# Layer 1 of a graph attention network: ELU from two Relus, softmax denominators over 125 partitions, last head in two pieces

## The reference

```python
h = (layernorm(x) @ W1).reshape(n, 8, 96)
e = leaky_relu(al_s[src] + al_d[dst], 0.2)
ex = exp(e - m[dst])                       # m: largest e into a node
z = segment_sum(ex, dst)
alpha = ex / (z[dst] + 1e-16)
out = segment_sum(h[src] * alpha, dst)     # a node, a head: 96 features
g = elu(out + b1)                          # input of layer 2
```

## Time and profile before

| | us |
|---|---|
| median of 3 runs | 1564.95 (1560.58 to 1566.44) |
| the profiled execution | 1564.78 |
| its span, first to last instruction | 1563.1 |
| TensorE busy (share of the span) | 1370.7 (88%) |
| VectorE busy | 1170.5 (75%) |
| ScalarE busy | 725.6 (46%) |
| GpSimd busy | 492.1 (31%) |

### The profile page before, as it was taken

The page is one execution under the profiler, slowest core; times in us unless marked ns, Lnnn a source line. Parts: engine busy times, 40 slices in busy tenths (PEclk is TensorE's granted clock), DMA queues, the critical chain, the costliest instruction groups (busy, mean ns, idle before and its releaser), DMA issues. The chain is left out here.

```text
span 1563.1 us, 30173 instructions
## 1 busy us (share of the span) xinstructions
PE 1370.7 (88%) x7656; PEld 1136.4 (73%) x7667; DVE 1170.5 (75%) x1821; ACT 725.6 (46%) x1160; POOL 492.1 (31%) x554
## 2 busy tenths in 40 slices
PE   6888988887777858889985999999999999999995
PEld 3656656732223327889984899999999999988995
DVE  5479999899999986858877566555566655787882
ACT  3465565354444442522223455444454544655662
POOL 1000000003333320022322445554454545555553
PEclk9899999799999997999986999999999999999998
DMA  4300001041221213233566988877788887999974
GB/s 166 134 17 10 17 18 69 19 172 59 71 92 59 79 38 121 82 105 101 124 174 199 285 212 211 233 176 166 178 198 222 198 211 171 231 285 276 260 173 82
DMA packets 100373, 222.55 MB, mean 142 GB/s; under 512 B 15068, under 2 KB 54236, under 8 KB 100200
## 3 DMA queue, kind: packets, MB, share of 16 engines
q1 hardware_dynamic: 77304, 141.00, 27.8%
q0 software_dynamic: 22240, 78.63, 24.6%
q10 hardware_dynamic: 784, 2.36, 0.4%
HBM read 162.27 MB, written 55.75 MB: 139 GB/s over the span
## 5 line engine op out<-in xcount | busy, mean ns | idle before, releaser
L934 PE MATMUL ps_o<-prob,h_head 128*97 128x512 f32 (+1 forms) x480 | 191.1, 538 | 56.0 <-DVE prob L877 56.0
L1969 POOL DMA_INDIRECT out_nodes<-y,to_index x92 | 154.5, 1679 | 217.9 <-DMA out_nodes<-y,to_index 184.1
L2254 PE MATMUL ps_h<-e_hi,e_xt_hi 128*128 (+1 forms) x546 | 193.9, 355 | 10.1 <-ACT e_xt_hi L2073 6.0
L934 PEld LDWEIGHTS ps_o<-prob,h_head 128*97 128x97 f32 x480 | 74.6, 167 | 172.8 <-issue 93.0
L2239 PE MATMUL ps_y<-e_hi,e_ht_hi 128*128 (+1 forms) x546 | 191.1, 350 | 8.0 <-issue 5.7
L2254 PE MATMUL ps_h<-e_lo,e_xt_hi 128*128 (+1 forms) x546 | 185.6, 340 | 0.0
L2239 PE MATMUL ps_y<-e_hi,e_ht_lo 128*128 (+1 forms) x546 | 183.7, 336 | 0.0
L2239 PE MATMUL ps_y<-e_lo,e_ht_hi 128*128 (+1 forms) x546 | 183.6, 336 | 0.0
L2137 DVE TENSOR_TENSOR e_lo<-raw,e_hi (+1 forms) x189 | 175.6, 953 | 5.4 <-ACT e_hi L2081 4.7
L790 ACT ACTIVATE score<-score,al_col 128x1250 f32<-128x1250 f32 x80 | 106.8, 1337 | 122.6 <-DVE score L841 122.4
L2090 ACT ACTIVATE y<-ps_y,gate 128x768 f32 (+1 forms) x91 | 82.2, 904 | 169.9 <-PE ps_y L2239 139.2
(11 more groups left out here) (322 smaller groups left out, 3096.2 us busy)
## 6 DMA issues: line engine op xcount, KB each, us to landing
raw<-in_ew SPq DMA_DIRECT2D x192, 384.0 KB
w_room<-rel_dram SPq DMA_DIRECT2D x14, 640.0 KB, 4.4
b_all<-in_eb SPq DMA_DIRECT2D x32, 192.0 KB
al_src<-al_dram SPq DMA_DIRECT2D x1, 5000.0 KB, 14.8
xs<-in_x SPq DMA_DIRECT2D x5, 768.0 KB, 13.0
x_in_t<-in_x SPq DMA_DIRECT2D x10, 384.0 KB, 3.5
out_nodes<-x SPq DMA_DIRECT2D x10, 384.0 KB, 4.0
table<-xf SPq DMA_DIRECT2D x10, 384.0 KB, 2.5
```

The source lines that it names most:

```text
L934: turn = nc.tensor.matmul(ps_o[u][0:C1 + 1, c, 0:WID[c]], h_head[:, u, t, :], prob[:, t % 2, 512 * c:512 * c + WID[c]], start=(t == 0), st ...
L1969: nc.gpsimd.indirect_dma_start(out, bass.IndirectOffsetOnAxis(to_index[:, w:w + 1], 0), y[:, w, :], None, bounds_check=ROWS - 1, compute_o ...
L2254: nc.tensor.matmul(ps_h[:, 0:HID], xt_hi[:, c, :], b[:, bass.ds(e % 2, 1), c * HID:(c + 1) * HID] .rearrange("p o m -> p (o m)"), start=(c ...
```

## The change

ELU in heads 0 to 6: ScalarE, after Exp, computes Relu(1 - exp) in `neg_t` and Relu(out + bias) in `out_t`, and VectorE subtracts the first from the second; before, VectorE took min and add of the exponential, then add and max.

Denominators of heads 0 to 6: `z_rows` has 125 partitions of 10 instead of 10 of 125; the addition of 1e-16 is a two-input instruction (z + 1e-16, max with z).

Last head: the row of denominators is turned by TensorE into ten columns (128x10), inverted on VectorE, and spread onto 96 partitions by ten further turns into the free accumulator `ps_o` 0; it no longer passes through DRAM. Scaling, Exp, ELU, the store and the terms run in two column pieces, 0 to 512 and 512 to 1250. The ELU is the old one there.

```diff
         wa_now = sb("wa2_now", [C1, 2, 3 * WIDE_AL])
-        z_rows = sb("z_rows", [NT, 2, N // NT])
+        ZP = N // NT
+        z_rows = sb("z_rows", [ZP, 2, NT])
+        z_cols = sb("z_cols", [P, 2, NT])
+        LAST = ((0, 4 * P), (4 * P, N))
...
+        rest_made, z_turned, z_step, z_spread = sem("rest_made"), sem("z_turned"), sem("z_step"), sem("z_spread")
...
     def store_g(h, u):
-        sp.wait_ge(elued, h + 3)
         now = g_head[:, u, :].rearrange("p (t n) -> p t n", n=P)
-        for k in range(h * C1 // P, (h * C1 + C1 - 1) // P + 1):
-            a, b = max(h * C1, k * P), min(h * C1 + C1, k * P + P)
-            for first, end in (((0, 2), (2, NT)) if h == H1 - 1 else ((0, NT),)):
+        for n, (first, end) in enumerate(((0, 4), (4, NT)) if h == H1 - 1 else ((0, NT),)):
+            sp.wait_ge(elued, h + 3 + n)
+            for k in range(h * C1 // P, (h * C1 + C1 - 1) // P + 1):
+                a, b = max(h * C1, k * P), min(h * C1 + C1, k * P + P)
                 sp.dma_start(s.g[a - k * P:b - k * P, first:end, k, :],
                              now[a - h * C1:b - h * C1, first:end, :]).then_inc(g_out, 16)
                 stored.append(stored[-1] + 16)
...
         sp.dma_start(s.z_dram.ap()[h:h + 1, :], out_t[C1:C1 + 1, u, 0:N]).then_inc(z_out, 16)
         sp.wait_ge(z_out, 16 * h + 16)
         sp.dma_start(z_rows[:, u, :], s.z_dram.ap()[h:h + 1, :]
-                     .rearrange("o (a b) -> (o a) b", a=NT)).then_inc(z_in, 16)
+                     .rearrange("o (a b) -> (o a) b", a=ZP)).then_inc(z_in, 16)
         sp.wait_ge(z_done, 2 * h + 2)
-        sp.dma_start(s.zi_dram.ap()[h:h + 1, :].rearrange("o (a b) -> (o a) b", a=NT),
+        sp.dma_start(s.zi_dram.ap()[h:h + 1, :].rearrange("o (a b) -> (o a) b", a=ZP),
                      z_rows[:, u, :]).then_inc(zi_out, 16)
         sp.wait_ge(zi_out, 16 * h + 16)
         sp.wait_ge(scaled, h + 1)
...
             sp.dma_start(w2_raw[:, 0:late, :], w2_rows[:, 0:late, :]).then_inc(w2_in, 16)
         if h >= 1:
             store_g(h - 1, 1 - h % 2)
-        reciprocal_sums(h, h % 2)
+        if h < H1 - 1:
+            reciprocal_sums(h, h % 2)
     store_g(H1 - 1, 1)
     for u in range(2):
-        sp.wait_ge(scale_in[u], 16 * (H1 // 2))
+        sp.wait_ge(scale_in[u], 16 * (H1 // 2 - u))
     sp.wait_ge(count_out, 16)
     sp.wait_ge(g_out, store_end[H1 - 1])
...
         act.wait_ge(elued, h + 2)
         nc.scalar.activation(neg_t[:, 0:N], out_t[0:C1, u, 0:N], ACT.Exp,
                              bias=bias_col[:, bass.ds(h, 1)]).then_inc(neg_exped, 1)
+        act.wait_ge(neg_exped, h + 1)
+        nc.scalar.activation(neg_t[:, 0:N], neg_t[:, 0:N], ACT.Relu, bias=1.0, scale=-1.0)
+        nc.scalar.activation(out_t[0:C1, u, 0:N], out_t[0:C1, u, 0:N], ACT.Relu,
+                             bias=bias_col[:, bass.ds(h, 1)]).then_inc(rest_made, 1)
+
+    def exp_last():
+        act.wait_ge(elued, H1 + 1)
+        for n, (a, b) in enumerate(LAST):
+            act.wait_ge(scaled, H1 + 2 + n)
+            nc.scalar.activation(neg_t[:, a:b], out_t[0:C1, 1, a:b], ACT.Exp,
+                                 bias=bias_col[:, H1 - 1:H1]).then_inc(neg_exped, 1)
...
         split_w2(k)
-    exp_out(H1 - 1, 1)
+    exp_last()
...
     def invert_sums(h, u):
         dve.wait_ge(z_in, 16 * h + 16)
-        nc.vector.tensor_scalar(z_rows[:, u, :], z_rows[:, u, :], 1e-16, None,
-                                ALU.add).then_inc(z_done, 1)
+        nc.vector.scalar_tensor_tensor(z_rows[:, u, :], z_rows[:, u, :], 1e-16, z_rows[:, u, :],
+                                       ALU.add, ALU.max).then_inc(z_done, 1)
         dve.wait_ge(z_done, 2 * h + 1)
         nc.vector.reciprocal(z_rows[:, u, :], z_rows[:, u, :]).then_inc(z_done, 1)
...
                                 ALU.mult).then_inc(scaled, 1)
     def elu(h, u):
-        dve.wait_ge(neg_exped, h + 1)
-        nc.vector.tensor_scalar(neg_t[:, 0:N], neg_t[:, 0:N], 1.0, -1.0, ALU.min,
-                                ALU.add).then_inc(neg_made, 1)
-        dve.wait_ge(neg_made, h + 1)
+        dve.wait_ge(rest_made, h + 1)
         dve.wait_ge(pads_set, 2)
         dve.wait_ge(al_added, h + 1)
-        nc.vector.scalar_tensor_tensor(g_head[:, u, :], out_t[0:C1, u, :], bias_col[:, bass.ds(h, 1)],
-                                       neg_t[:, :], ALU.add, ALU.max).then_inc(elued, 1)
+        nc.vector.tensor_tensor(g_head[:, u, :], out_t[0:C1, u, :], neg_t[:, :],
+                                ALU.subtract).then_inc(elued, 1)
+
+    def invert_last():
+        dve.wait_ge(z_turned, 1)
+        nc.vector.tensor_scalar(z_cols[:, 0, :], ps_r[:, 0:NT], 1e-16, None, ALU.add).then_inc(z_step, 1)
+        dve.wait_ge(z_step, 1)
+        nc.vector.reciprocal(z_cols[:, 1, :], z_cols[:, 0, :]).then_inc(z_step, 1)
+
+    def scale_last():
+        for n, (a, b) in enumerate(LAST):
+            dve.wait_ge(z_spread, n + 1)
+            nc.vector.tensor_tensor(out_t[0:C1, 1, a:b], out_t[0:C1, 1, a:b], first_flat[0:C1, a:b],
+                                    ALU.mult).then_inc(scaled, 1)
+
+    def elu_last():
+        dve.wait_ge(al_added, H1)
+        for n, (a, b) in enumerate(LAST):
+            dve.wait_ge(neg_exped, H1 + n)
+            nc.vector.tensor_scalar(neg_t[:, a:b], neg_t[:, a:b], 1.0, -1.0, ALU.min,
+                                    ALU.add).then_inc(neg_made, 1)
+            dve.wait_ge(neg_made, n + 1)
+            end = NP if b == N else b
+            nc.vector.scalar_tensor_tensor(g_head[:, 1, a:end], out_t[0:C1, 1, a:end],
+                                           bias_col[:, H1 - 1:H1], neg_t[:, a:end],
+                                           ALU.add, ALU.max).then_inc(elued, 1)
...
     over_heads(dve, head)
     for k in range(3):
         split_w2(k)
-    invert_sums(H1 - 1, 1)
-    for k in range(3, KD):
+    invert_last()
+    split_w2(3)
+    scale_last()
+    for k in range(4, KD):
         split_w2(k)
-    scale_out(H1 - 1, H1 // 2 - 1, 1)
-    elu(H1 - 1, 1)
+    elu_last()
...
         pe.wait_ge(wa_set, h + 1)
         pe.wait_ge(elued, h + 3)
         for c, (at, width) in enumerate(PARTS):
+            if last and c == 1:
+                pe.wait_ge(elued, H1 + 3)
             turn = nc.tensor.matmul(ps_al[0:HIGH_AL, 0:width],
                                     wa_now[:, u, c * HIGH_AL:(c + 1) * HIGH_AL],
                                     g_head[:, u, at:at + width], start=False,
...
         return turn
...
     over_heads(pe, head)
+    pe.wait_ge(rel_kept, 3)
+    pe.wait_ge(pads_set, 2)
+    pe.wait_ge(out_kept, H1 + 2)
+    for t in range(NT):
+        turn = nc.tensor.transpose(ps_r[:, t:t + 1], out_t[C1:C1 + 1, 1, t * P:(t + 1) * P],
+                                   s.ident[C1:C1 + 1, C1:C1 + 1])
+    turn.then_inc(z_turned, 1)
+    pe.wait_ge(z_step, 2)
+    for t in range(NT):
+        turn = nc.tensor.transpose(first_flat[0:C1, t * P:(t + 1) * P],
+                                   z_cols[:, 1, t:t + 1].broadcast_to([P, C1]), s.ident[:, :])
+        if t in (3, NT - 1):
+            turn.then_inc(z_spread, 1)
     add_terms(H1 - 1, 1, last=True).then_inc(al_summed, 1)
...
```

## The result

| | before, us | after, us |
|---|---|---|
| median | 1565.7 (1560.58 to 1573.64) | 1549.41 (1549.09 to 1552.4) |
| ratio | | 0.9903, interval 0.9883 to 0.9923 |
| profiled execution, and its span | 1564.78, 1563.1 | 1549.09, 1547.4 |
| layer 1 by head | 293.4 | 275.3 |
| last kept sums to last copies of the terms | 19.71 | 11.85 |

The kernel is faster by 16 us, 1.0% (12 to 18 by the interval); 1545.4 was forecast, with 1539 to 1553. The layer's length is worked out as the start of the second layer's first instruction (595.71 and 576.58) less that of VectorE's operation on `bend` near the layer's start (302.32 and 301.25). It went down by 18.1 us against 19.4 forecast. The second layer begins 19.1 us sooner, of which 1.1 us lie ahead of layer 1, in code that is the same. At the end 16 are left.

What follows compares the result with a forecast made beforehand. VectorE was taken to set the pace in the heads, single transfers and operations at the layer's end. ELU 6.1, denominators 5.9 and last head 7.4 sum to 19.4 us off 1564.95: 1545.4 us, range 1539 to 1553.

Steps and rivals of the forecast that it cites:

- What bounds the layer: Heads of layer 1: VectorE, busy 167.7 of 168.6 us, sets the pace; what leaves its queue shortens the stage one for one.
- ELU: Heads 0 to 5: one subtraction on VectorE replaces its 2.41 us of steps, saving 1.01 us a head, 6.1 us in all.
- The Relus' room: ScalarE behind each Exp in the loop: two Relus end about 471.1, 1.2 us before VectorE wants them, so cost nothing.
- Denominators: Addition and reciprocal in heads 0 to 6: 0.7 us saved in two heads, 0.9 in five, 5.9 us (3.9 to 6.3).
- The Trainium skill's rule on the shared port: At the denominators: two-input VectorE instructions and GpSimd's SBUF reads exclude each other; the reciprocal lets GpSimd in, same 5.9 us.
- Transfers in small pieces: Denominators through DRAM in 125 pieces of 40 bytes: landing in about 1.5 us, costing nothing; skill-page estimate 6.3 us.
- The last head: End of layer 1: turns on TensorE and two column pieces end the terms at 586.4 against 593.84, 7.4 us saved.
- The carrying to the end: Whole kernel: stages have barriers behind them, so one ending earlier starts the next earlier; all 19.4 us counted at the end.
- (a): End of layer 1: TensorE's clock stays at 2.4 GHz, 2 to 4 us more gain, 1542 us; chance 0.10.
- (b): Heads: GpSimd is shut out, h_head comes late and VectorE stops 3.5 us in five heads, about 1559 us; chance 0.06.
- (c): Heads: the Relus are late; at twice their duration VectorE waits 1.5 us in seven heads, 1556 us; chance 0.05.
- (d): Denominators' small-piece transfers land late, from 5.5 us: 1563 us at 8, 1608 at 14.5; chance 0.05 up to 8, 0.04 above.

Runs made afterwards that it cites:

- the other chip: The kernel before and the changed kernel, both unchanged, measured once more on another chip: 1566.79 us (ratio 0.9997) and 1551.63 us (0.9899).

## Why the prediction was right, point by point

- **What bounds the layer**: right. VectorE had 0.2 us of idle time in 160.9, and each edit on it shortened the heads by what it took off.
- **ELU**: 1.01 a head forecast, 1.01 measured (33.72 to 32.71); 6.1 for six, 6.07 by head 6's scaling. The Relus' room was put at 1.2 us and is 1.56, since from the Exp's start they end 3.84 us later instead of 4.3. In the last head the subtraction waits 1.17 us (1.7 was forecast), and that costs nothing: from head 6's scaling to its terms it is 7.14 us before (565.56 to 572.70) and after (554.29 to 561.43).
- **Denominators**: the term that was mis-sized. 5.9 forecast for heads 0 to 6, 4.1 measured: 0.57 and 0.71 in the two heads without the copy (1.4 forecast) and 2.8 in the five with it, 0.55 each (4.5 forecast). The step that failed is "I expect the copy to get in between the addition and the reciprocal". The addition ends 0.03 us behind the copy (450.24 and 450.21), so it is the copy that goes first, the case that the prediction priced at 0.5 as its low end. The uncontended pair is cheaper than put, 0.34 instead of 0.4, but the score behind it takes up to 0.1 more to the next start.
- **The Trainium skill's rule on the shared port** (SBUF, State Buffer, section Who interferes with whom): that the two exclude each other agrees, since the addition beside the copy takes 1.10 us and without it 0.17. The prediction read from it that an addition with two inputs lets no copy in ahead. The rows show the copy ahead of it as ahead of the one-input form (1.10 and 1.13 us). By the recorded starts the addition was 0.09 us the earlier, and it still waited, so these starts don't tell which of the two gets the port.
- **Transfers in small pieces**: nothing was counted, and nothing is to be seen in the layer. They land 0.24 to 0.27 us later (1.47 against 1.23 for the write, 1.65 against 1.38 for the read), where 5.5 us were free. The estimate that the prediction worked out from the Trainium skill's page DMA: Bandwidth & Descriptors, 6.3 us with five engines, is not borne out: 1.5 and 1.65 us were measured. No row shows the number of engines; what fails is the scaling of the whole 1.5 us with the pieces of each.
- **The last head**: 7.4 forecast, 7.9 measured, of which 6.1 by the turns. The turns took 0.77 us for ten, 0.08 each and so less than the 0.11 to 0.23 assumed, the spreads 0.13 each; the terms took 4.45 at the low clock, as assumed from the earlier trace rows. Most of the half microsecond more lies in the turns: the scaling began 2.8 us behind the kept sums, where 3.3 was forecast, and the ELU ended 8.7 behind them (571.63), where 9.2 was.
- **The carrying to the end**: "a stage that ends earlier starts the next one earlier" holds for the starts, 19.1 us at the second layer and 21.2 at the experts' first rows (847.39 to 826.21). The prediction then took the end to move with the start, and 5.5 us of the 21.2 didn't arrive, which it doesn't foresee. Luck hid a part of this. The profiled execution of after began layer 1 1.1 us sooner, and in its second layer TensorE's granted clock was back at 1.00 some 8.2 us after the start instead of 10.3, and the stage was 2.0 us shorter. Neither is owed to the change: on the other chip it is 10.2 us in both kernels, and the second layers take 99.1 and 99.0. So 18.1 + 1.1 + 2.0 - 5.5 = 15.7 us between the profiled executions, against 19.4 forecast. The range held, with 1549.4 in 1539 to 1553, and the forecast was 4.0 us too low.
- **The rivals**: (a) fell, the clock was at 0.55 in the terms. (b) fell: GpSimd's copies got in, and TensorE's products waited for nothing but VectorE's, as the group below shows (those of 512 columns; the others show no wait). (c) fell, with 1.56 us of room; with two more operations on ScalarE it came true, at 0.9 to 1.0 us a head. (d) fell: 0.27 us later, against the 5.5 at which it began.

The group of the heads' products in after (idle time behind the second bar, with what ended it):

```profile
L972 PE MATMUL ps_o<-prob,h_head 128*97 128x512 f32 x296 | 144.4, 610 | 47.0 <-DVE prob L914 47.0
```

## What to carry to other kernels

Where one engine fills a stage, cost each edit from its start to the next start on that engine; the parts, made alone, added up here to the whole within 0.1 us by the last head's start, and what moves to another engine is free up to the room ahead of its reader, which is to be read from the trace and is used up at once behind it. A short transfer through DRAM that only turns a row into columns was worth replacing by TensorE here, where nothing overlaps it (6.1 us for two ways there and back). Don't take a gain early in a long kernel for a gain at the end: read the later stages' lengths too, in more than one execution of each kernel. The experts took 5.5 of 21.2 us back here, and a further 5.3 us in the layer did not show in a whole time whose interval is 12 us wide.

## What was not expected of the hardware

- GpSimd's copy of `h_head`, which stands behind the starved one below, gets in ahead of the small instruction that ends VectorE's chain of two-input operations, be it of one input (1.13 us) or two (1.10 us instead of 0.17), and costs VectorE 0.93 us for its own 0.98.
- The same chain starves GpSimd: its copy of 96x6 elements takes 10.8 us in the group of after, as it took 11.5 before, and ends with the chain (438.52 and 10.77: 449.29, 0.07 behind the last product). That isn't so at every boundary in such a chain: the copy at 342.64 got in at once, beside a score. What decides is open.

```profile
L745 POOL COPY wa_now<-wa 96x6 f32 x6 | 64.6, 10763 | 133.9 <-PE ps_al L986 133.9
```

- A transfer of 125 pieces of 40 bytes lands only 0.24 to 0.27 us later than one of 10 pieces of 500 bytes.
- A reciprocal over 125x10 is 0.22 us, over 10x125 0.93, for the same 1250 elements: the time goes by the columns, and twelve times the partitions cost nothing that shows.
